# Weights made inside the edge tables, fewer waits on TensorE, and edge rows gathered two pairs behind one wait

## What is computed

```
mean(h)[i] = sum of h[src] over the edges with dst == i, over max(count, 1)
conv(h)    = mean(h) @ Wl + b + h @ Wr          # Wl.T and Wr.T in the first block

h = relu(conv(x; a1));  x1  = layernorm(x  + conv(h; a2))          # 128 -> 128 -> 128
h = relu(conv(x1; b1)); h = relu(conv(h; b2));
out = layernorm(x1 + conv(h; b3))                                   # 128 -> 256 -> 256 -> 128
```

## Time and profile before

| | us |
|---|---|
| median of three runs (5244.66 to 5256.48) | 5248.4 |
| the profiled execution's own time | 5245.4 |
| its span in the trace | 5243.1 |
| PE busy | 4825.3 |
| DVE busy | 3541.0 |
| POOL busy | 2605.3 |
| ACT busy | 2571.6 |

### The profile page before, as it was taken

One profiled execution on the slowest core, in us unless ns is written; L12 is line 12 of the kernel. 1 busy time (PEld: TensorE's weight loads), 2 busy tenths in 40 slices (PEclk: granted clock), 3 DMA queues, 4 the chain that ended last, 5 costly groups with the idle time before them and its releaser, 6 DMA issues. The chain is left out here.

```text
span 5243.1 us, 154819 instructions
## 1 busy us (share of the span) xinstructions
PE 4825.3 (92%) x40438; PEld 4697.6 (90%) x40439; DVE 3541.0 (68%) x10023; ACT 2571.6 (49%) x7254; POOL 2605.3 (50%) x3137
## 2 busy tenths in 40 slices
PE   1688878899999799999989999999999899999999
PEld 0577777799999799999989999999999799999999
...
GB/s 28 125 175 172 171 168 170 184 226 238 235 230 235 151 204 204 205 205 204 198 165 177 177 177 179 176 177 178 179 176 173 166 237 235 238 237 234 237 236 203
DMA packets 1247004, 1007.21 MB, mean 192 GB/s; under 512 B 69844, under 2 KB 1177713, under 8 KB 1246902
## 3 DMA queue, kind: packets, MB, share of 16 engines
...
## 5 line engine op out<-in xcount | busy, mean ns | idle before, releaser
L1320 ACT ACTIVATE f_ring_b<-f_e_product_b,t_rec_all 128x256 f32 (+1 forms) x784 | 328.7, 470 | 897.9 <-PE f_e_product_b L1275 808.8
L1247 PE MATMUL f_product_b<-b_r_all,f_t_hi_b 128*128 128x256 f32 x2352 | 725.8, 309 | 5.8 <-DVE f_onehot_b L1363 5.6
L1178 POOL TENSOR_TENSOR f_held_b<-ones_all 1x1 f32<-1x1 f32 x382 | 74.3, 195 | 1187.8 <-ACT f_e_idx_b L1300 1079.4
L1251 PE MATMUL f_product_b<-b_r_all,f_t_lo_b 128*128 128x256 f32 x2352 | 664.1, 282 | 0.0
L1249 PE MATMUL f_product_b<-b_r_all,f_t_hi_b 128*128 128x256 f32 x2352 | 662.2, 282 | 0.0
L938 DVE TENSOR_TENSOR m_onehot_a<-iota_all,t_win_all 128x512 fp32r<-128x512 f32 (+3 forms) x784 | 485.4, 620 | 251.4 <-PE m_product_a L814 168.8
L1315 ACT ACTIVATE f_t_hi_b<-f_turned_b 128x512 fp32r<-128x512 f32 x588 | 330.4, 597 | 605.2 <-PE f_turned_b L1219 326.7
L1254 PE MATMUL f_product_b<-f_ring_b,f_onehot_b 128*128 x3136 | 626.0, 280 | 0.0
L1355 DVE SCALAR_TENSOR_TENSOR f_t_lo_b<-f_turned_b,f_t_hi_b 128x512 fp32r<-128x512 f32 x588 | 387.5, 687 | 352.7 <-ACT f_t_hi_b L1315 343.0
L806 PE MATMUL m_product_a<-a_r_all,m_t_full_a 128*128 128x128 f32 x3136 | 590.3, 275 | 0.0
L938 DVE TENSOR_TENSOR m_onehot_b<-iota_all,t_win_all 128x512 f32<-128x512 f32 (+1 forms) x392 | 250.3, 639 | 498.7 <-PE m_product_b L814 498.7
...
## 6 DMA issues: line engine op xcount, KB each, us to landing
g<-f_rows_out_b SPq DMA_DIRECT2D x392, 512.0 KB
f_rows_in_b<-g SPq DMA_DIRECT2D x196, 512.0 KB
m_rows_in_b<-g SPq DMA_DIRECT2D x196, 512.0 KB
m_t_full_a<-in_x_flat_dram SPq DMA_DIRECT2D x196, 256.0 KB
h<-m_rows_out_a SPq DMA_DIRECT2D x196, 256.0 KB
m_rows_in_a<-h SPq DMA_DIRECT2D x196, 256.0 KB
m_res_in_a<-in_x_dram SPq DMA_DIRECT2D x196, 256.0 KB
x<-m_rows_out_a SPq DMA_DIRECT2D x196, 256.0 KB
```

Source lines behind the costliest of these rows:

```text
L1247: pe.matmul(to, t_hi[:, s, k, cols], cv["r2"][:, k, 0, :], start=(t % per == 0 and k == 0), stop=False, skip_group_check=True)
L1251: pe.matmul(to, t_lo[:, s, k, cols], cv["r2"][:, k, 0, :], start=False, stop=False, skip_group_check=True)
```

## The change

1. The block of `weights` is gone. A class `Weights` does its work inside the block of `edge_tables`: its 20 loads are issued by SP behind the loads of the scan, its transposes and bias matmuls stand first on PE, ACT makes the copies and high parts, DVE clears two tiles before its first wait and makes the low parts after L221. l2 exists only for the wide layers, bias_row only for the narrow ones. The ten loads of r_src and r_dst move from SP's queue to ACT's, and SP waits for three cleared tiles, not five.
2. PE no longer waits in `multiply` for the ring (but for the last groups), for the sum, and for the second compare apart from the first: the head waits for both. `project` no longer waits for the copied edges but in the last pair. In `wide_pass` the head's wait for the low part of the nodes goes too.
3. `take_numbers` hands over the numbers of two pairs, at odd p. POOL waits, marks and gathers two pairs at odd p, so that the gathers of an even pair are issued one step later than before. In b3 the bias is added to the residual before the gathers of the step, not behind them.

```diff
+    def loads(self, sp):
+        for i, cv in enumerate(self.convs):
+            kt, fo = cv["w"], cv["f_out"]
+            raw, brow = self.raws[:, i, :, :], self.brows[:, i, :]
+            for m, key in enumerate(("Wl", "Wr")):
+                if cv["turned"]:
+                    sp.dma_start(raw[:, m, 0:P], cv[key]).then_inc(self.s_in[i].sem, 16)
+                else:
+                    sp.dma_start(raw[:, m, 0:kt * fo].rearrange("p (k n) -> p k n", k=kt),
+                                 cv[key].rearrange("(k p) n -> p k n", p=P)).then_inc(self.s_in[i].sem, 16)
+            for n in range(2):
+                sp.dma_start(brow[n:n + 1, 0:fo], cv["b"].rearrange("(a n) -> a n", a=1)).then_inc(self.s_in[i].sem, 16)
+
+    def turns(self, pe):
+        for i, cv in enumerate(self.convs):
+            pe.wait_ge(self.s_in[i].sem, 64)
+            if cv["turned"]:
+                for m in range(2):
+                    pe.transpose(self.sides(i)[m], self.raws[:, i, m, 0:P], self.pr.ident[:, :])
+            pe.matmul(self.spread_bias(i), self.pr.ones[:, :], self.brows[0:1, i, 0:cv["f_out"]], start=True,
+                      stop=True).then_inc(self.s_pe.sem, 1)
+
+    def copies(self, act):
+        act.wait_ge(self.s_zero.sem, 1)
+        act.wait_ge(self.s_pe.sem, len(self.convs))
+        for i, cv in enumerate(self.convs):
+            act.wait_ge(self.s_in[i].sem, 64)
+            left, right = [t.rearrange("p (k n) -> p k n", k=cv["w"]) for t in self.sides(i)]
+            act.activation(cv["l32"][:, :, :], left, ACT.Copy)
+            act.activation(cv["r32"][:, :, :], right, ACT.Copy)
+            act.activation(cv["bias"][:, :], self.spread_bias(i), ACT.Copy)
+            if "l2" in cv:
+                act.activation(cv["l2"][:, :, 0, :], left, ACT.Copy)
+            else:
+                act.activation(cv["bias_row"][:, :, :], self.zero[:, :, :], ACT.Copy)
+            act.activation(cv["r2"][:, :, 0, :], right, ACT.Copy).then_inc(self.s_out.sem, 1)
+
...
+    def low_parts(self, v):
+        done = 0
+        for i, cv in enumerate(self.convs):
+            v.wait_ge(self.s_out.sem, i + 1)
+            v.tensor_tensor(cv["r2"][:, :, 1, :], cv["r32"][:, :, :], cv["r2"][:, :, 0, :].bitcast(F32), ALU.subtract)
+            if "l2" in cv:
+                v.tensor_tensor(cv["l2"][:, :, 1, :], cv["l32"][:, :, :], cv["l2"][:, :, 0, :].bitcast(F32), ALU.subtract)
+                continue
+            brow = self.brows[:, i, 0:P]
+            v.tensor_copy(self.b_hi[:, :], brow).then_inc(self.s_mid.sem, 1)
+            v.wait_ge(self.s_mid.sem, done + 1)
+            v.tensor_tensor(self.b_lo[:, :], brow, self.b_hi[:, :].bitcast(F32), ALU.subtract).then_inc(self.s_mid.sem, 1)
+            v.wait_ge(self.s_mid.sem, done + 2)
+            v.tensor_scalar(self.b_lo[:, :], self.b_lo[:, :], self.pr.ident[0:2, 1:2], None,
+                            ALU.mult).then_inc(self.s_mid.sem, 1)
+            v.wait_ge(self.s_mid.sem, done + 3)
+            for n in range(T):
+                ins = v.scalar_tensor_tensor(out=cv["bias_row"][0:2, n, :], in0=self.b_hi[:, :].bitcast(F32),
+                                             scalar=self.pr.ident[0:2, 0:1], in1=self.b_lo[:, :],
+                                             op0=ALU.mult, op1=ALU.add)
+            ins.then_inc(self.s_mid.sem, 1)
+            v.wait_ge(self.s_mid.sem, done + 4)
+            done += 4
...
             def scan_layout(tile, shift):
 
                 lo = 1 if shift < 0 else 0
                 if shift < 0:
-                    load(tile[0:1, 1:C], dst1[0:C - 1].rearrange("(a n) -> a n", a=1))
+                    load(sp, tile[0:1, 1:C], dst1[0:C - 1].rearrange("(a n) -> a n", a=1))
                 a, b = lo, full
-                load(tile[a:b, :], dst1[a * C + shift:b * C + shift].rearrange("(p n) -> p n", n=C))
+                load(sp, tile[a:b, :], dst1[a * C + shift:b * C + shift].rearrange("(p n) -> p n", n=C))
                 left = rest - max(shift, 0)
-                load(tile[full:full + 1, 0:left],
+                load(sp, tile[full:full + 1, 0:left],
                      dst1[full * C + shift:full * C + shift + left].rearrange("(a n) -> a n", a=1))
 
             for tile, shift in ((d_here, 0), (d_prev, -1), (d_next, 1)):
                 scan_layout(tile, shift)
-            for tile, arr in ((r_src, src1), (r_dst, dst1)):
-                for b in range(RB):
-                    n = min(P, rows_full - b * P)
-                    load(tile[0:n, b, :], arr[b * P * P:(b * P + n) * P].rearrange("(p n) -> p n", n=P))
-                b, p = rows_full // P, rows_full % P
-                load(tile[p:p + 1, b, 0:rest_q], arr[rows_full * P:E].rearrange("(a n) -> a n", a=1))
+            weights.loads(sp)
             sp.wait_ge(s_v.sem, K_REC)
...
                              rec_view[b * P * P:(b * P + n) * P].rearrange("(p n) -> p n", n=P)
                              ).then_inc(s_rec.sem, 16)
+
+        @block.scalar
+        def _(act):
+            act.wait_ge(s_fill.sem, 5)
+            for tile, arr in ((r_src, src1), (r_dst, dst1)):
+                for b in range(RB):
+                    n = min(P, rows_full - b * P)
+                    load(act, tile[0:n, b, :], arr[b * P * P:(b * P + n) * P].rearrange("(p n) -> p n", n=P))
+                b, p = rows_full // P, rows_full % P
+                load(act, tile[p:p + 1, b, 0:rest_q], arr[rows_full * P:E].rearrange("(a n) -> a n", a=1))
+            weights.copies(act)
         N_LOADS = len(n_loads)
 
         @block.vector
...
@@ -220,6 +343,7 @@
                                  ALU.is_equal), 23)
             step(v.scalar_tensor_tensor(out=r_out[:, :, :], in0=r_end[:, :, :], scalar=float(NOWHERE),
                                         in1=r_dstf[:, :, :], op0=ALU.mult, op1=ALU.add), 24)
+            weights.low_parts(v)
             v.wait_ge(s_rec.sem, 16 * (1 + RB))
             v.wait_ge(s_pe.sem, 5)
             for n, (table, bank) in enumerate(((pr.t_src, 0), (pr.t_dst, 1), (pr.t_rec, 2), (pr.t_out, 3))):
@@ -228,6 +352,7 @@
 
         @block.tensor
         def _(pe):
+            weights.turns(pe)
             pe.wait_ge(s_v.sem, 6)
             pe.matmul(pc[0:1, 0:P], first[:, C - 1:C], pr.ident[:, :], start=True, stop=True).then_inc(s_pe.sem, 1)
             pe.matmul(pc[0:1, P:2 * P], last[:, 0:1], pr.ident[:, :], start=True, stop=True).then_inc(s_pe.sem, 1)
...
@@ -729,19 +766,20 @@
                                    ALU.add).then_inc(s_biased.sem, 1)
 
             def step(g, p):
-                if p is not None and (p.reg is not None or p.off + D < G):
-                    wait(pool, s_index, p.n(D + 1))
-                    wait(pool, s_held, p.n(1))
+                if biased and g is not None:
+                    add_bias(g)
+                if p is not None and p.off % 2 == 1 and (p.reg is not None or p.off + D < G):
+                    wait(pool, s_index, p.plus(D + 1).turn(2))
+                    wait(pool, s_held, p.plus(1).turn(2))
                     mark().then_inc(s_held.sem, 1)
+                    gather(p.plus(D - 1))
                     gather(p.plus(D))
                 if norm and split and has(g, 1):
                     mix(g.plus(-1))
-                if biased and g is not None:
-                    add_bias(g)
 
             mark().then_inc(s_held.sem, 1)
...
                 return slots + columns
 
             def multiply(g, at, u):
+
                 s, r = g.slot(2), g.slot(R)
                 if u == 0:
-                    wait(pe, s_onehot, g.n(0, 2) + 1)
+                    wait(pe, s_onehot, g.n(1, 2))
                     if flat is not None:
                         wait(pe, rows_here[r], g.turn(R) + 1)
                     else:
                         wait(pe, s_full, g.n(1, kt))
-                    wait(pe, s_ring, min(g.off + LEAD - 2, G) if g.reg is None else g.n(LEAD - 2))
-                    wait(pe, s_sum, g.n(-1))
+                    if rings_end(g):
+                        wait(pe, s_ring, G)
                     if norm and not split and not biased:
                         pe.matmul(product[s][:, :], pr.two_rows[:, :],
                                   cv["bias_row"][:, :, :].rearrange("p a n -> p (a n)"),
@@ -809,7 +848,6 @@
                     pe.matmul(both, onehot[:, s, t, :], ring[:, bass.ds(at[t] * (C * fo), C * fo)],
                               start=False, stop=False, skip_group_check=True)
                 if u == 1:
-                    wait(pe, s_onehot, g.n(0, 2) + 2)
                     for n in range(FIRSTS, WINDOWS):
                         mm = pe.matmul(product[s][:, bass.ds(at[n + EXTRAS] * (C * fo), C * fo)], onehot[:, s, n, :],
                                        ring[:, bass.ds(at[n] * (C * fo), C * fo)],
@@ -818,7 +856,8 @@
 
             def project(p):
                 s = p.slot(2)
-                wait(pe, s_efull, p.n(1))
```

(18 more changed lines are left out.)

191 lines of the change are left out of this document (79 added, 112 removed).

## The result

The changed kernel takes 5430.4 us (median of 4 runs, 5413.34 to 5440.49) against 5249.35 us before: a ratio of 1.034, with a 95% interval of 1.031 to 1.037. It is 181 us slower. The forecast was 5132 us.

A forecast was written before the change was run, and what follows sets the result against it. PE was taken as the bound, nearly full in most passes and in a1 waiting for its own instruction stream; 5245.4 less 30 (setup) and 85 (waits) gave 5130.4, stated as 5132 us, range 5095 to 5200.

The forecast's parts named there:

- Pairs on POOL: POOL's gathers, four behind one mark, the even group's issued one group later: cost 0, saved marks worth 0.
- the compare or the pairs late: Outcome in which DVE's second compare or POOL's paired gathers come late: chance 0.07, of which 0.05 above the old time.
- The slower rival: PE's head in b1 waits for DVE's second compare, 1.17 us past its cover: 229 us in b1 alone, 5361 us.
- The waits: Fewer waits in PE's instruction stream in all passes but b3: 85 us gained, 55 of them in a1.
- what is late next takes it back: Bound on a1's gain from fewer waits: only 20 us if PE's wait for ACT's L856 takes most back.
- The setup: Weights made inside the edge tables instead of in their own block: 30 us gained, bounds 20 and 36.
- The low parts: DVE's low parts and bias rows inside the edge tables: 9 us, of which 3 stick out of a 6.31 us hole.
- PE's turns of the weights: PE's weight turns, ahead of its L232 in the edge tables, wait for all 20 loads: +2 us, bounds 0 and +4.
- The ACT table load: ACT's table load of 1.28 us moves off the path of the first gather: -0.6 us, bounds 0 and -1.3.
- +3 + 2 - 1.8: Setup terms: DVE's low parts +3 us, PE's weight turns +2, loads of r_src and r_dst on ACT's queue -1.8.
- a1's period above 3.7 us: Sign against the forecast: if a1's time per group stays above 3.7 us, the waits were hidden.
- hidden waits: Rival: PE's instruction stream runs ahead, so satisfied waits cost nothing and only the setup's 30 us come: 5216 us, chance 0.15.

The follow-up runs named there:

- e3_pairs: The kernel before with the third part alone: numbers for two pairs at once, four gathers behind one mark; 5508.61 us, ratio 1.048.
- e7_setup_waits: The changed kernel with POOL's and ACT's part as before, so setup and waits without the pairs; 5221.53 us, ratio 0.995.
- e10_after_true_spread: The changed kernel with one pair gathered at each step, POOL also waiting at even steps for ACT's copy of the turned edges; 5173.61 us, ratio 0.986.
- e2_waits: The kernel before with the second part alone: PE's waits removed, the head waiting for both compares; 5249.6 us, ratio 1.000.
- e12: The kernel before with POOL's gathers of the edges' rows replaced by plain loads of the same size on the same queue; 5052.81 us, ratio 0.963.
- e11: The changed kernel with POOL's gathers of the edges' rows replaced by plain loads of the same size on the same queue; 4994.7 us, ratio 0.952.
- e1_setup: The kernel before with the first part alone: the weights made inside the edge tables; 5207.45 us, ratio 0.993.
- e9_true_spread: The kernel before with numbers handed over for two pairs, one pair gathered at each step, POOL waiting at even steps for ACT's edge copy; 5214.77 us, ratio 0.994.

## Why the prediction was wrong

**The step that failed** is *Pairs on POOL*: "Cost 0", with the argument that POOL has room and that 15 us lie between issue and use. Both are true: beyond the starts of the passes PE never waited for a gather's data. But the gathers also act on something that they share with PE: from its start until up to some 2 us later, signals of PE's matmuls are held back. Four in a row cost 262 us (e3_pairs). With setup and waits changed as well it is less: 5430 less the 5222 of e7_setup_waits, 209 us. None of my rivals was this one; the 0.07 for "the compare or the pairs late" named the pairs, but only the compare had a price. The slower rival put the loss on DVE's second compare; L1295, the head in b1, does wait for that now:

```profile
PE f_product_b L1295 <- DVE f_onehot_b L1412: 9.4, 37, 1.4
```

But this is 9.4 us of the 35 that b1 lost, and it goes with the late signals: with the gathers spread and the same waits (e10_after_true_spread) that wait is 0.4 us and b1 takes 870 us.

The trace of before held the evidence: 20.6 us (L871) and 38.4 us (L879) of ACT's waits in a1 are put down to "remote", and some 800 signals were late. I took those rows for waits of an engine that isn't the bound.

**The waits.** Forecast 85 us, 55 of them in a1; measured none (e2_waits, 1.000). The mechanism is there: issue ahead of the head fell by 19 us in 700, a third of the 55. The other step, that what is late next takes it back, was a bound of mine and not my value: the ring's low part took 29 us and the copy of the edges 10. In a1 of the kernel before, the projection's signal was late in 62 of 187 groups and that of the turned edges in 74 of 187. With no late signals (e12 to e11) a1 gives 21 us and all passes 27; the pairs, as plain loads, are in that number too, so that 27 us is the most that the runs give for the waits, not a measurement of them alone. Even then the term was mis-sized by two thirds. My reading: register instructions and satisfied waits at 0.1 us each are hidden as long as something else is later. a2, b1 and b2 got 6 us together there, where 30 were forecast. The Trainium skill's rule of the wait queue (Perfetto Trace Analysis, "Tensor Engine Instruction (MATMUL, LD_WEIGHTS)") would have given the right time for e2_waits, but its reason isn't what the trace shows: the stream did get shorter, and waits for other engines took its place.

**The setup.** Forecast 30 us, measured 39 (e1_setup), 34 of them before the first gather. The low parts took 8.7 us (42.58 to 51.26) for the 9 that I reckoned, and L350 starts at 51.30, 1.6 us later than its forerunner at 49.67. DVE's first step came 2.05 us earlier (24.41 for 26.46; I took 1.8), which is in line with what the Trainium skill states in DMA: Bandwidth & Descriptors, "Issuing engines are not separate DMA queues". PE's turns of the weights took back 1.2 us of that, where I had put 2: DVE's sixth step ends at 28.80, but PE is in the bias matmuls until 30.15 and L357 starts at 30.08; L232 had started at 30.91, 0.06 us behind DVE. The lines for it:

```profile
27.22 2.93 PE L142 MATMUL w_spread_all<-b_row_all,ones_all 1*128 1x128 f32 x8
...
27.83 0.97 DVE L316 TENSOR_TENSOR_SCAN last_all<-key_all 128x392 f32<-128x392 f32 x1
```

The ACT table load of 1.28 us left the path, and the first gather follows the start of ACT's pass by 0.8 us (109.54 to 110.37) instead of 4.2 (140.58 to 144.80): there I had counted 0.6 us of 3.4. The rest of the way, +3 + 2 - 1.8, came to +1.6. Another 14 us came in a1 (735 for 749), though its code was unchanged, and I can't put them down to a place.

**What would show it.** I had named a1's period above 3.7 us as the sign of hidden waits. It rose to 4.07 (700 us over 172 groups). That the waits were hidden is right (e2_waits), but the sign said nothing of a loss.

**Open.** By what POOL's indirect DMA holds PE's signals isn't shown; the runs show when, for whom (PE's, not ACT's or DVE's where there is a record or a free reader) and that plain loads from the same queue don't. Why the spread of e9_true_spread makes a1 24 us shorter than before isn't shown either; fewer of its projection signals are late there (38 of 187 for 62 of 187), but e1_setup's a1 is 14 us shorter than before as well, without any change to the gathers. Why the change to four in a row costs time in a1, where such rows were common before, is argued from the projection's signals alone.
